# A Flamingo layer with routed experts: the rows of one token tile put per step behind the second norm, and the router's selection in front of the row maximum

## The reference

```python
x = x + jnp.tanh(g_xattn[0]) * xattn(layernorm(x), ctx)         # softmax over 64 keys, 16 heads
x = x + jnp.tanh(g_ffn[0]) * ffn(layernorm(x))

# ffn(x):
scores = jax.nn.sigmoid(x @ W_gate_router)
_, sel = jax.lax.top_k(scores + expert_bias, 2)
w = take_along_axis(scores, sel, axis=1); w = w / (w.sum(-1, keepdims=True) + 1e-20)
shared = jax.nn.silu(x @ Wg_s) * (x @ Wu_s) @ Wd_s
out = shared + sum over the two selected experts e of
      w_e * ((jax.nn.silu(x @ Wg[e]) * (x @ Wu[e])) @ Wd[e])
```

## Time and profile before

| | |
|---|---|
| time, median of 3 runs | 340.79 us (337.12 to 341.66) |
| the profiled execution's own time | 341.64 us |
| its span, first to last instruction | 339.9 us |
| mean granted TensorE clock, share of full speed | 0.925 |
| busy: PE | 287.4 us (85%) |
| busy: DVE | 254.9 us (75%) |
| busy: POOL | 161.2 us (47%) |
| busy: ACT | 143.3 us (42%) |
| step 5 begins (PE's L1302) | 87.57 us |
| step 14 begins (PE's L1311) | 174.13 us |
| the last put | 203.84 us |

### The profile page before, as it was taken

How to read it: one execution, slowest core, us unless ns; L and a number is a source line. 1 busy time by engine, 2 the same in 40 slices (tenths; PEclk the granted TensorE clock), 3 DMA queues, 4 the chain that set the end, 5 groups by cost and what they waited for, 6 DMA issues and landing times.

```text
span 339.9 us, 6401 instructions
## 1 busy us (share of the span) xinstructions
PE 287.4 (85%) x1792; PEld 259.9 (76%) x1793; DVE 254.9 (75%) x672; ACT 143.3 (42%) x349; POOL 161.2 (47%) x208
## 2 busy tenths in 40 slices
PE   3968979999989989969678848798999999999660
PEld 2957768999978888959577748697898989999440
DVE  1687898999999998869785673269766667776586
ACT  1471653555655655635353323543344344444100
POOL 7022023356638888884876554029343434343400
PEclk9997998999999999979987996789999999999755
DMA  6790003011112222211100144023333343331768
GB/s 189 276 355 12 0 0 95 1 48 47 49 46 78 95 93 79 74 53 48 63 32 33 47 156 145 16 66 94 96 108 111 84 122 96 114 105 43 243 220 278
DMA packets 28892, 33.23 MB, mean 98 GB/s; under 512 B 3688, under 2 KB 25538, under 8 KB 28866
## 3 DMA queue, kind: packets, MB, share of 16 engines
q1 hardware_dynamic: 22706, 21.82, 21.5%
q0 software_dynamic: 3408, 8.46, 7.1%
q10 hardware_dynamic: 2752, 2.63, 2.4%
HBM read 21.14 MB, written 12.67 MB: 99 GB/s over the span
## 4 chain that ended last, share of the span: by engine, by line
PE 52%; DVE 21%; POOL 10%; issue 8%; ACT 3%; DMA 3%; SPq 1%; DVEq 0%; POOLq 0%; ACTq 0%
PE bank L1234 9%; PE bank L1236 8%; PE bank L1235 8%; PE scores_ps L1234 6%; PE scores_ps L1235 5%; PE scores_ps L1236 5%; POOL rows_dram L544 4%; DMA x_sb<-in_x_dram 3%; PE bank L1382 3%; POOL probs L573 2%; PE bank L1221 2%; DVE probs L1052 2%; DVE row_sum L1030 2%; DVE pT_lo L1025 2%; DVE x_sb L1144 2%
## 5 line engine op out<-in xcount | busy, mean ns | idle before, releaser
L624 POOL DMA_INDIRECT routed_dram<-probs,sct_idx x39 | 38.4, 986 | 68.8 <-DVE probs L1131 67.2
L1236 PE MATMUL bank<-AB_hi,pT_lo 128*128 128x256 f32 (+1 forms) x206 | 59.4, 289 | 0.0
L573 POOL TENSOR_TENSOR probs<-probs,row_inv 128x1024 f32<-128x1024 f32 x16 | 30.5, 1904 | 35.1 <-DVE row_inv L1034 35.1
L1236 PEld LDWEIGHTS bank<-AB_hi,pT_lo 128*128 128x128 f32 (+1 forms) x206 | 40.8, 198 | 0.0
L1234 PE MATMUL bank<-AB_hi,pT_hi 128*128 128x256 f32 x128 | 39.1, 306 | 0.0
L1235 PE MATMUL bank<-AB_lo,pT_hi 128*128 128x256 f32 x128 | 37.7, 295 | 0.0
L544 POOL DMA_INDIRECT rows_dram<-xn,slot_i x32 | 31.9, 996 | 11.3 <-issue 8.9
L1234 PE MATMUL scores_ps<-AB_hi,xnT_hi 128*128 128x512 f32 x64 | 26.4, 412 | 3.2 <-DVE xnT_lo L1014 3.2
L1234 PE MATMUL bank<-AB_hi,pT_lo 96*128 x78 | 25.2, 323 | 2.0 <-DVE pT_lo L1134 1.9
L1234 PEld LDWEIGHTS bank<-AB_hi,pT_hi 128*128 128x128 f32 x128 | 26.4, 206 | 0.1
L1235 PEld LDWEIGHTS bank<-AB_lo,pT_hi 128*128 128x128 f32 x128 | 26.1, 204 | 0.1
(11 more groups left out here) (222 smaller groups left out, 839.7 us busy)
## 6 DMA issues: line engine op xcount, KB each, us to landing
probs<-rows_dram SPq DMA_DIRECT2D x30, 130.0 KB, 2.2
x_sb<-in_x_dram SPq DMA_DIRECT2D x2, 1024.0 KB, 9.6
AB_free<-routed_dram SPq DMA_DIRECT2D x4, 512.0 KB, 5.6
AB_free<-routed_dram SPq DMA_DIRECT2D x8, 256.0 KB, 4.6
out_dram<-x_sb ACTq DMA_DIRECT2D x8, 256.0 KB, 2.2
raw_buf<-in_L_ffn_Wg_dram SPq DMA_DIRECT2D x8, 192.0 KB, 2.5
raw_buf<-in_L_ffn_Wu_dram SPq DMA_DIRECT2D x8, 192.0 KB, 3.0
raw_buf<-in_L_ffn_Wd_dram SPq DMA_DIRECT2D x4, 384.0 KB, 3.5
```

Source lines behind the costliest of these rows:

```text
L573: nc.gpsimd.tensor_tensor(pr, pr, row_inv[:, :].unsqueeze(2).to_broadcast([P, H, KV]), ALU.mult).then_inc(norm_done, 1)
L624: nc.gpsimd.indirect_dma_start(routed_dram[:, :], bass.IndirectOffsetOnAxis(ap=sct_idx[(k - 2) % (2 * RING)][:, 0:1], axis=0), y_sb[ks][:, ...
L1236: return nc.tensor.matmul(out_ap, a_lo, b_hi, start=False, stop=last)
```

## The change

Two things move; no instruction is added or taken away on DVE, PE, ACT or SP, and POOL issues the same 32 indirect transfers, in the same order of tiles.

On POOL the puts of step t stood at the end of the step, behind the low part of the weights, in portions: tile 0 in step 6, tile 1 in step 7, tiles 2 and 3 in step 8, tile 4 in step 9, tiles 5 and 6 in step 10, none in step 11, tiles 7 and 8 in step 12, and tiles 9, 10 and 11 in steps 13, 14 and 15. Now one tile is put in each of steps 6 to 15, between the factors of the second norm and the multiplication of the probabilities: tile t-6 in steps 6 to 13, tile 8 in step 14, tile 10 in step 15. Tiles 9 and 11 follow at the end of steps 14 and 15. Tiles 12 to 15 follow the loop, as before.

On DVE the selection moves from behind the subtraction to the place between the shared expert's gate and the row maximum.

```diff
--- before.py
+++ after.py
@@ -544,12 +544,12 @@
                     nc.gpsimd.indirect_dma_start(rows_dram[:, :], bass.IndirectOffsetOnAxis(ap=slot_i[:, t, k:k + 1], axis=0),
                                                  xn2[:, t % KEEP, :], None).then_inc(rows_put[t % KEEP], 16)
 
-            def put_batch(b, part=slice(None)):
-
+            def put_tile(t):
+
+                b = [t < z for _, z in BATCHES].index(True)
                 pool.wait_ge(slot_done, b + 1)
                 pool.wait_ge(payload_done, b + 1)
-                for t in list(range(*BATCHES[b]))[part]:
-                    put_rows(t)
+                put_rows(t)
 
             def second_norm(w):
 
@@ -566,6 +566,8 @@
                 w, m = t - 1, t + 1
                 if inside(w):
                     second_norm(w)
+                if 6 <= t < T:
+                    put_tile(t - 6 if t < T - 2 else 2 * t - 20)
                 if inside(m):
 
                     pool.wait_ge(inv_done, m + 1)
@@ -585,29 +587,13 @@
                     pool.wait_ge(wd_hi_done, n + 1)
                     nc.gpsimd.tensor_tensor(Wd_lo[:, part, :], raw_d[n % 2][:, :, :],
                                             Wd_hi[:, part, :].bitcast(F32), ALU.subtract).then_inc(wd_lo_done, 1)
-                if t == 6:
-                    put_batch(0, slice(0, 1))
-                if t == 7:
-                    put_batch(0, slice(1, 2))
-                if t == 8:
-                    put_batch(0, slice(2, 4))
-                if t == 9:
-                    put_batch(1, slice(0, 1))
-                if t == 10:
-                    put_batch(1, slice(1, 3))
-                if t == 12:
-                    put_batch(2, slice(0, 2))
-                if t == 13:
-                    put_batch(2, slice(2, 3))
-                if t == 14:
-                    put_batch(3, slice(0, 1))
-                if t == 15:
-                    put_batch(3, slice(1, 2))
+                if T - 2 <= t < T:
+                    put_tile(2 * t - 19)
 
             token_loop(step, between)
             second_norm(T - 1)
-            put_batch(4)
-            put_batch(5)
+            for t in range(BATCHES[4][0], T):
+                put_tile(t)
 
             def late_add(z):
                 pool.wait_ge(late_read, z + 1)
@@ -1039,6 +1025,9 @@
                         place(b)
                 if inside(v):
                     hidden(v)
+                for b, (_, z) in enumerate(BATCHES):
+                    if z + 1 == t:
+                        choose(b)
                 if inside(u):
 
                     dve.wait_ge(scores_done, u + 1)
@@ -1052,9 +1041,6 @@
                     nc.vector.tensor_tensor(prob[q][:, :].rearrange("p (h k) -> p h k", k=KV), sc,
                                             row_max[:, :].unsqueeze(2).to_broadcast([P, H, KV]),
                                             ALU.subtract).then_inc(sub_done, 1)
-                for b, (_, z) in enumerate(BATCHES):
-                    if z + 1 == t:
-                        choose(b)
                 if inside(t):
                     second_norm(t)
 
```

## The result

The changed kernel takes 351.06 us (median of 4 runs, 350.43 to 351.54), the kernel before beside it 341.23 us (337.12 to 343.35). The ratio is 1.033 with a 95% interval of [1.024, 1.042]: **slower**, where I had forecast 338.0 us and given slower by over 2% a chance of 0.04. The profiled execution took 351.54 us, 9.9 more than the one before, and its span is 349.8 us instead of 339.9.

The account below looks back on a forecast made before the run. DVE's 7.78 us loop through ACT was taken to bound the token loop, close behind PE. A 0.5 us loss to step 13, then later gains, put the end 2.8 us earlier: 338.0 us against 340.79, range 333.5 to 342.

Parts of the forecast that it names:

- Moved: the selection: DVE's loop: selection ahead of the subtraction costs 0.6 us more each time; gain from PE's rank waits priced at nothing.
- The 0.6 us a time for the place: DVE's loop: extra cost per selection, because nothing of the loop runs beside it in the new place.
- The sign that I had named for being wrong: DVE's gate of step 13 ending well before 166 or after 169 us would show the forecast wrong.
- Port contention: POOL's puts beside DVE: 0.96 us per transfer also in the new place, since low parts are not locking operations.
- The clock: PE, rival: waits of about 1.6 us lower the clock behind three of them, +4.5 us to 342.5; chance 0.13.
- Added: a wait in step 6: POOL's first put waits for DVE's places, so PE starts step 7 about 1.6 us late, once.
- Removed: POOL's lateness: POOL's factors follow their statistics directly; PE's waits of 3.00, 3.02 and 2.08 us ahead of L1281 go.
- The upper end of this part: Token loop, if PE alone counted: 12 to 13 us won; not taken, because DVE can't follow.
- The sum: Along DVE's loop: step 13's gate 0.5 us later, then tile 15's residual and the rest 2.8 us earlier; median 338.0 us.

Follow-up runs that it names:

- E: Edit: minimum and maximum of a token's two expert numbers by one-input tensor_reduce instead of two-input tensor_tensor; alone on the kernel before 339.89 us.
- the pair of the first put: Two kernels with one-input minimum and step 6's tile 0 put behind POOL's multiplication: POOL's half alone 333.57 us, whole change 336.85 us.
- e11: Kernel before with DVE's half alone (selection ahead of the row maximum) and one-input minimum and maximum: 340.44 us, ratio 1.003.
- e1: Changed kernel with the one-input minimum and maximum of the expert numbers: 334.38 us, ratio 0.988.
- e2: Kernel before with DVE's half alone, the selection ahead of the row maximum, two-input minimum kept: 343.73 us, ratio 1.011.
- e5: Kernel before with POOL's half alone (moved puts) and the one-input minimum and maximum: 335.21 us, ratio 0.984.
- e4: Control: kernel before with only the one-input minimum and maximum: 339.89 us, ratio 1.0005.
- e3: Kernel before with POOL's half alone: moved puts, selection behind the subtraction, two-input minimum kept: 334.72 us, ratio 0.984.
- the probe: Kernel before plus a tiny unused DVE minimum of two SBUF inputs in steps 2 to 15, ahead of the row maximum: 348.26 us, ratio 1.025.

## Why the prediction was wrong, step by step

- **Moved: the selection** is the step that failed. I took 2.7, 2.5, 2.5 and 2.4 us for the selections, the durations of the old place, into a place where other work runs beside them. From the first instruction to the start of the row maximum they lasted 96.59 - 92.54 = 4.05, and then 4.86, 5.54 and 5.23 us. With E they last 2.7, 2.4, 2.4 and 2.1 us, my durations or a little less. The 0.6 us a time for the place was too much, and that is a matter of size: the pair of the first put shows 0.3, e11 none. The sign that I had named for being wrong, a gate of step 13 that ends after 169, came: it ends at 176.24.
- **Port contention**: I weighed the Trainium skill's rule (SBUF — State Buffer, Who interferes with whom) for the puts only, and the puts are indeed innocent: 0.96 to 1.24 us, and a minimum of 0.17 beside them. The section says besides that a DVE instruction with two SBUF inputs contends with a GpSimd instruction that reads SBUF, and that a reduction never does; the trace agrees in both (3.27 and 0.17 us). I looked for what the change did to POOL's transfers and not for what it did to the 16 instructions that it moved on DVE.
- The kernel before showed it already. Its minimum lasted between 170 and 549 ns (in its line: min/median/max, first and last start, forms):

```profile
L913 DVE TENSOR_TENSOR bank<-top_e x6: 170/173/549, 97.3 to 197.6; 128x2 f32<-128x2 uint32 x3, 128x3 f32<-128x3 uint32 x2, 128x4 f32<-128x4 uint32 x1
```

  The 549 is the one at 173.75 us, which ended with POOL's low part. A spread by a factor of 3 in the duration of one small instruction was the sign, and I had not asked for it.
- **The clock** was a rival with 0.13 at 342.5 us, to be decided by waits of about 1.6 us. Those of 2.55 and 1.54 us left the clock at 1.00 in steps 6 and 7; behind those of 3.35 and 4.06 us it fell, which cost 2.80 and 2.30 us. A part of the loss, and a consequence: with the hold gone (e1), all steps to 14 run at 1.00. But the length of a wait doesn't decide it: in e2 a wait of 2.56 us left 1.00 in step 6, and one of 2.53 was followed by 0.83 in step 9; in the POOL half with E (e5) one of 1.33 was followed by 0.85 in step 6.
- **Added: a wait in step 6** was right: 1.54 us where I said 1.6.
- **Removed: POOL's lateness** was right: no wait ahead of L1267 in steps 7 to 13, though 1.74 us in step 14. The put was undersized: I had 2.4 us from the factors to its end, and it is 2.9 (in step 11 from 150.64 to 153.53), because 0.56 us pass before the first transfer. In steps 8, 11 and 13 the multiplication so begins 1.0 to 1.2 us behind the inverse instead of 0.5. PE doesn't feel it, but it moves POOL's two long operations 0.5 to 0.7 us further under the selection's minimum. The upper end of this part was also added up wrong: steps 11, 13 and 14 give 12.8 us by themselves, with the waits of steps 6 and 9 (1.34 and 0.93 us) 15.0 and not 12 to 13.
- **The sum**, tested without the hold: my forecast was a loop shorter by 2.8 us, and e1's is 114.3 instead of 117.6, 3.3 shorter. Its profiled execution took 334.1 us where I had 338.8. Beside those 0.5 us, step 5 begins 1.6 us earlier (85.97 for 87.57), and the part behind the loop takes 132.2 us instead of 134.8. Neither is the change: e4, the kernel before but for E, has 85.72 and 131.8 us there, and the POOL half (e3) 87.72 and 135.0. As a ratio to before, my 338.0 of 340.79 is 0.992, inside e1's interval of 0.978 to 0.999: without the hold nothing speaks against the sum, though an interval of 2% is a weak test of it.
- The loss adds up. Between the changed kernel and e1 the loop is 127.1 - 114.3 = 12.8 us longer: 10.1 of hold and 5.1 of clock in steps 9 and 12, the 15.2 us that steps 5 to 14 are longer, less 2.4 given back behind step 14. That is 9.5 us over the loop of before, of the 9.9 between the two spans.

## What to carry to other kernels

When an instruction moves, ask what runs on the other engines over its new place, not only what its own engine and its waiters do there. On DVE, give every moved operation with two SBUF inputs (and every copy from SBUF to SBUF) the duration of the POOL operation that it lands on (of two, where they follow each other), and prefer a reduction over one strided input where it computes the same. In a profile look at the minimum and maximum duration of small operations: a stall of this kind appears as busy time, and neither in the waits nor in the idle time.

## What the runs showed of the hardware

- A `tensor_tensor` of 128x2 to 128x4 elements with both inputs in SBUF, alone 0.16 to 0.17 us, lasts to the end of a POOL `TENSOR_TENSOR` of 128x768, 96x1024 or 128x1024 elements that is running: 1.49 us under one of 1.91, up to 3.33 us through two in a row. POOL isn't slowed (1.90 to 1.92 us). For the probe uint32 instead of float32 inputs, 128x3 instead of 128x4 elements (one run) and an output in PSUM make no difference: 1.49 or 1.50 us.
- A DVE copy of 128x8 floats from SBUF to SBUF is held likewise (1.50 us). The selection's own copies have an input in PSUM; they (0.17 us), reductions (0.17) and a `tensor_tensor` with one input in PSUM (0.22) weren't held beside a POOL operation that went on for another 0.7 us or more (e1, step 5).
- POOL's issue of indirect transfers and its operations on 128x1 elements held nothing visible (0.16 to 0.20 us beside them).
- A held operation mostly gets in between two of POOL's operations, even where the second has had all its inputs for 2.7 us; three times in each of two kernels it didn't (2.65, 3.27 and 3.33 us; 2.64, 3.30 and 3.33), for a reason that stays open.
